# A complex mix of heads and the second step of a forward transform: fp32 matmuls against three fp16 passes of high and low halves

## The reference, cut to what matters

```python
xf = jnp.fft.fft2(x)
qf = xf.reshape(b, HEADS, hd, h * w)
qn = _l2norm_lastdim(qf)
attn_f = jnp.einsum('bhcn,bhdn->bhcd', qn, qn) * temp_f[None]
attn_f = jax.lax.complex(jax.nn.softmax(attn_f.real, axis=-1), jax.nn.softmax(attn_f.imag, axis=-1))
out_cplx = jnp.einsum('bhcd,bhdn->bhcn', attn_f, qf)
out_f = jnp.abs(jnp.fft.ifft2(out_cplx)).reshape(b, c, h, w)
g = jax.nn.sigmoid(_conv(g, w2, b2))
out_f_l = jnp.abs(jnp.fft.ifft2(g * xf))
```

## Time and profile before

| | |
|---|---|
| median of 3 runs | 26842.19 us (26841.0 to 26844.8) |
| the profiled execution | 26840.82 us, of which the span is 26839.0 us |
| PE busy | 23909.5 us (89%) |
| DVE busy | 19661.7 us (73%) |
| ACT busy | 13616.0 us (51%) |
| granted clock of TensorE, mean | 0.939 |

### The profile page before, as it was taken

One profiled execution on the slowest core, in us unless ns is written; L12 is line 12 of the kernel. 1 busy time (PEld: TensorE's weight loads), 2 busy tenths in 40 slices (PEclk: granted clock), 3 DMA queues, 4 the chain that ended last, 5 costly groups with the idle time before them and its releaser, 6 DMA issues. The chain is left out here.

```text
span 26839.0 us, 328765 instructions
## 1 busy us (share of the span) xinstructions
PE 23909.5 (89%) x108001; PEld 14269.1 (53%) x108001; DVE 19661.7 (73%) x22753; ACT 13616.0 (51%) x19703; POOL 12340.1 (46%) x4613
## 2 busy tenths in 40 slices
PE   6988989889898998989988888888888888888888
PEld 4776867768677676877733333333333333333333
DVE  3562635537255372644699999999999999999999
ACT  1413223131321413214277777777777777777777
POOL 0000000000000000000099999999999999999998
PEclk7998989989898998989999999999999999999999
DMA  1121121211202112021244444444444444444444
GB/s 53 49 76 61 33 65 38 76 61 42 66 32 73 61 55 69 27 66 57 75 178 165 193 165 173 183 167 191 169 169 185 169 191 166 167 189 167 190 168 163
DMA packets 816277, 3112.23 MB, mean 116 GB/s; under 512 B 61865, under 2 KB 325434, under 8 KB 530362
## 3 DMA queue, kind: packets, MB, share of 16 engines
q1 hardware_dynamic: 815802, 3106.12, 31.1%
HBM read 2813.61 MB, written 292.30 MB: 116 GB/s over the span
## 5 line engine op out<-in xcount | busy, mean ns | idle before, releaser
L2176 POOL TENSOR_TENSOR hid<-hid,bc 128x2048 f32<-128x2048 f32 x2048 | 7814.6, 3816 | 909.2 <-DVE carry L2082 906.5
L1845 PE MATMUL yp<-hid,ident 128*128 128x512 f32 x16384 | 7344.7, 597 | 430.7 <-POOL hid L2176 430.7
L2150 POOL TENSOR_SCALAR_AFFINE_SELECT ident<-ident 128x128 f32<-128x128 f32 x1 | 0.3, 294 | 13331.3 <-DVE ident L2035 13331.3
L1845 PEld LDWEIGHTS yp<-hid,ident 128*128 128x128 f32 x16384 | 3039.7, 189 | 4628.3 <-issue 3957.9
L2068 DVE TENSOR_TENSOR_SCAN hid<-da,carry,t 128x512 f32<-128x512 f32 x3968 | 4857.8, 1266 | 111.0 <-DVE carry L2082 7.7
L2074 DVE TENSOR_TENSOR_SCAN hid<-t,carry,hid 128x512 f32<-128x512 f32 x3968 | 4828.1, 1258 | 29.2 <-ACT t L1916 28.5
L2169 POOL TENSOR_TENSOR hid<-bc,du 128x1024 f32<-128x1024 f32 x2048 | 4101.4, 2003 | 197.0 <-PE yp L1845 170.6
L1066 PE MATMUL bk<-region 128*128 128x256 f16 (+2 forms) x32688 | 3946.9, 279 | 24.6 <-ACT region L1365 19.1
L1066 PEld LDWEIGHTS bk<-region 128*128 128x128 f16 (+2 forms) x32688 | 3400.0, 119 | 603.9 <-issue 175.8
L1916 ACT ACTIVATE t<-delta,v_a 128x512 f32<-128x512 f32 x4096 | 2660.0, 681 | 1574.0 <-DVE hid L2074 1570.9
L1801 PE MATMUL pj<-xn,w_x 128*128 128x512 f32 x4096 | 2376.5, 734 | 1079.2 <-ACT xn L1941 1031.0
(11 more groups left out here) (272 smaller groups left out, 24892.0 us busy)
## 6 DMA issues: line engine op xcount, KB each, us to landing
bc<-bc_rows SPq DMA_DIRECT2D x1024, 2048.0 KB, 7.2
work<-in_shift_d SPq DMA_DIRECT2D x256, 512.0 KB, 3.5
xpad<-in_x SPq DMA_DIRECT2D x32, 2048.0 KB, 18.8
work<-in_x SPq DMA_DIRECT2D x128, 512.0 KB, 4.8
gated<-work SPq DMA_DIRECT2D x256, 256.0 KB, 2.2
region<-gated SPq DMA_DIRECT2D x256, 256.0 KB, 2.9
region<-heads SPq DMA_DIRECT2D x256, 256.0 KB, 3.1
region<-in_x SPq DMA_DIRECT2D x256, 256.0 KB, 3.6
```

Of the source, the lines that this page charges most:

```text
L1845: m = nc.tensor.matmul(yp[:, h, :], ident[:, :], hid[:, k % 4, n, :], start=False, stop=(g == G - 1 and n == 3), skip_group_check=True)
L2176: nc.gpsimd.tensor_tensor(hid[:, k % 4, :, :], hid[:, k % 4, :, :], bc[:, g, 1, :, :], ALU.mult).then_inc(s_hc.sem, 1)
```

## The change

An fp32 value, scaled by a power of two, is split into an fp16 high half and an fp16 low half (value less high half), and a product is made of three passes: high by high, weights high by data low, weights low by data high.

In the forward transform, ScalarE's copy to `AB` makes the high half; VectorE makes the low half by `ab_low` (one scalar_tensor_tensor from PSUM), ahead of `xi_copy` in each step. Stage1 and stage2 wait for the low half. Stage2 does 12 fp16 matmuls for 4 fp32 ones, with tables split once in the setup (`dft`). The copies to `XR` and `XI` scale back.

In the heads stage, ScalarE's shifted real copy and VectorE's shifted imaginary one make high halves (`imh` is the count of the latter), and VectorE makes both low halves. The copy of the turned rows moves from ScalarE to VectorE, between the lows and `add_squares`. The mix does 12 fp16 matmuls for 4 fp32 ones, with `mix16` split once per image; the squares scale back.

The diff, cut to its core (semaphore declarations are left out):

```diff
@@ -42,6 +42,8 @@
+HSCALE, HWEIGHT = 128.0, 16384.0
+ASCALE, CSCALE = 16.0, 16384.0
@@ -193,7 +195,9 @@
-        AB = wk(4096, 1024).rearrange("p (s c u) -> p s c u", s=2, u=P)
+        AB = wk(4096, 1024).bitcast(F16).rearrange("p (s h c u) -> p s h c u", s=2, h=2, u=P)
+        ab_flat = wk(4096, 1024).bitcast(F16).rearrange("p (s h n) -> p s h n", s=2, h=2)
+        dft = sb("dft16", [P, 2, 3 * P], F16)
@@ -203,7 +207,8 @@
-        shifted = [wk(1024 + 2048 * i, 1024) for i in range(2)]
+        shifted = [wk(1024 + 2048 * i, 1024).bitcast(F16).rearrange("p (c s n) -> p c s n", c=2, s=2) for i in range(2)]
+        mix16 = wk(10240, 3 * P).bitcast(F16).rearrange("p (i s o) -> p i s o", i=3, s=2)
@@ -407,6 +412,10 @@
+                    for i, part in enumerate((k["cs"], k["sc"][:, 0:P])):
+                        of_i = slice(2 * P * i, 2 * P * i + (2 - i) * P)
+                        link(nc.vector.tensor_scalar(dft[:, 0, of_i], part, CSCALE, None, ALU.mult))
+                        link(nc.vector.scalar_tensor_tensor(dft[:, 1, of_i], part, CSCALE, dft[:, 0, of_i], ALU.mult, ALU.subtract))
@@ -712,8 +723,14 @@
                 def xi_copy(t):
...
-                    V.tensor_copy(XLAST[:, 1, 4 * t:4 * t + 4], spectrum[:, :, U64])
-                    V.tensor_copy(XI[:, 4 * t:4 * t + 4, :], spectrum[:, :, 0:U64]).then_inc(s_xi.sem, 1)
+                    back_by = 1.0 / (ASCALE * CSCALE)
+                    V.tensor_scalar(XLAST[:, 1, 4 * t:4 * t + 4], spectrum[:, :, U64], back_by, None, ALU.mult)
+                    V.tensor_scalar(XI[:, 4 * t:4 * t + 4, :], spectrum[:, :, 0:U64], back_by, None, ALU.mult).then_inc(s_xi.sem, 1)
+
+                def ab_low(t):
+                    dve.wait_ge(s_s1.sem, s_s1.at(b, t + 1))
+                    dve.wait_ge(s_ab.sem, s_ab.at(b, t + 1))
+                    V.scalar_tensor_tensor(ab_flat[:, t % 2, 1], bk[t % 2][:, :], ASCALE, ab_flat[:, t % 2, 0], ALU.mult, ALU.subtract).then_inc(s_abl.sem, 1)
...
                 def columns(i):
@@ -722,9 +739,12 @@
                 columns(0)
+                ab_low(0)
                 columns(1)
...
                     for t in range(4 * i, 4 * i + 4):
+                        if t + 1 < NK:
+                            ab_low(t + 1)
...
                         columns(i + 2)
@@ -779,6 +799,8 @@
+                link(V.tensor_scalar(mix16[:, :, 0], mix_t[:, :, :], HWEIGHT, None, ALU.mult))
+                link(V.scalar_tensor_tensor(mix16[:, :, 1], mix_t[:, :, :], HWEIGHT, mix16[:, :, 0], ALU.mult, ALU.subtract))
@@ -795,6 +817,12 @@
+                def turned_rows(kk):
+                    dve.wait_ge(s_tr.sem, s_tr.at(b, kk + 1))
+
+                    dve.wait_ge(s_sh.sem, s_sh.at(b, kk))
+                    V.tensor_copy(turned, bk[0][:, :]).then_inc(s_trc.sem, 1)
+
                 def add_squares(kk):
@@ -802,10 +830,17 @@
                 def body(kk, par):
...
-                    V.tensor_copy(shifted[par][:, 512:], bk[2][:, :]).then_inc(s_shi.sem, 1)
+                    V.tensor_scalar(shifted[par][:, 1, 0], bk[2][:, :], HSCALE, None, ALU.mult).then_inc(s_imh.sem, 1)
+                    dve.wait_ge(s_shr.sem, s_shr.at(b, kk + 1))
+                    V.scalar_tensor_tensor(shifted[par][:, 0, 1], bk[1][:, :], HSCALE, shifted[par][:, 0, 0], ALU.mult, ALU.subtract)
+                    dve.wait_ge(s_imh.sem, s_imh.at(b, kk + 1))
+                    V.scalar_tensor_tensor(shifted[par][:, 1, 1], bk[2][:, :], HSCALE, shifted[par][:, 1, 0], ALU.mult, ALU.subtract).then_inc(s_shi.sem, 1)
+                    if not (isinstance(kk, int) and kk == NK - 1):
+                        turned_rows(kk + 1)
...
+                turned_rows(0)
@@ -1094,20 +1129,22 @@
                 def stage1(t):
...
-                    pe.wait_ge(s_ab.sem, s_ab.at(b, t - 1))
+                    pe.wait_ge(s_abl.sem, s_abl.at(b, t - 1))
...
                 def stage2(t):
-                    pe.wait_ge(s_ab.sem, s_ab.at(b, t + 1))
+                    pe.wait_ge(s_abl.sem, s_abl.at(b, t + 1))
...
-                    A, Bm = AB[:, t % 2, :, 0:HALF], AB[:, t % 2, :, HALF:]
-                    for o, (ca, cb_) in ((bk[2 + t % 2], (k["cs"][:, 0:P], k["cs"][:, P:])), (bk[4 + t % 2], (k["sc"][:, 0:P], k["cs"][:, 0:P]))):
+                    COS, NSIN, SIN = 0, P, 2 * P
+                    for o, (ca, cb_) in ((bk[2 + t % 2], (COS, NSIN)), (bk[4 + t % 2], (SIN, COS))):
...
-                        mm(o3, ca, A, start=True, stop=False)
-                        m = mm(o3[:, :, 1:64], cb_, Bm, start=False, stop=True)
+                        for wh, ph in ((0, 0), (0, 1), (1, 0)):
+                            mm(o3, dft[:, wh, ca:ca + P], AB[:, t % 2, ph, :, 0:HALF], start=(wh == 0 and ph == 0), stop=False)
+                        for wh, ph in ((0, 0), (0, 1), (1, 0)):
+                            m = mm(o3[:, :, 1:64], dft[:, wh, cb_:cb_ + P], AB[:, t % 2, ph, :, HALF:], start=False, stop=(wh == 1))
@@ -1195,11 +1232,11 @@
-                    re, im = shifted[par][:, 0:512], shifted[par][:, 512:]
-                    mm(o_re, mix_t[:, 0, :], re, start=True, stop=False)
-                    mm(o_re, mix_t[:, 2, :], im, start=False, stop=True)
-                    mm(o_im, mix_t[:, 0, :], im, start=True, stop=False)
-                    mm(o_im, mix_t[:, 1, :], re, start=False, stop=True).then_inc(s_o.sem, 1)
+                    for o, terms in ((o_re, ((0, 0), (2, 1))), (o_im, ((0, 1), (1, 0)))):
+                        for n_, (w_, part) in enumerate(terms):
+                            for wh, ph in ((0, 0), (0, 1), (1, 0)):
+                                m = mm(o, mix16[:, w_, wh, :], shifted[par][:, part, ph, :], start=(n_ == 0 and wh == 0 and ph == 0), stop=(n_ == 1 and wh == 1))
+                    m.then_inc(s_o.sem, 1)
...
                 def body(kk, par):
@@ -1380,13 +1417,14 @@
                 def xr_copy(t):
...
-                    cp(XLAST[:, 0, 4 * t:4 * t + 4], spectrum[:, :, U64])
-                    cp(XR[:, 4 * t:4 * t + 4, :], spectrum[:, :, 0:U64]).then_inc(s_xr.sem, 1)
+                    back_by = 1.0 / (ASCALE * CSCALE)
+                    cp(XLAST[:, 0, 4 * t:4 * t + 4], spectrum[:, :, U64], scale=back_by)
+                    cp(XR[:, 4 * t:4 * t + 4, :], spectrum[:, :, 0:U64], scale=back_by).then_inc(s_xr.sem, 1)
...
                 for t in range(NK):
...
-                    cp(AB[:, t % 2, :, :].rearrange("p c u -> p (c u)"), bk[t % 2][:, :]).then_inc(s_ab.sem, 1)
+                    cp(ab_flat[:, t % 2, 0], bk[t % 2][:, :], scale=ASCALE).then_inc(s_ab.sem, 1)
@@ -1433,18 +1471,12 @@
-                def turned_rows(kk):
-                    act.wait_ge(s_tr.sem, s_tr.at(b, kk + 1))
-
-                    act.wait_ge(s_sh.sem, s_sh.at(b, kk))
-                    cp(turned, bk[0][:, :]).then_inc(s_trc.sem, 1)
-
                 def squares(kk, par):
...
-                        cp(sq2[s], bk[3 + 2 * par + s][:, :], ACT.Square).then_inc(s_os.sem, 1)
+                        cp(sq2[s], bk[3 + 2 * par + s][:, :], ACT.Square, scale=1.0 / (HSCALE * HWEIGHT)).then_inc(s_os.sem, 1)
...
                 def root(kk):
@@ -1455,15 +1487,12 @@
-                    cp(shifted[par][:, 0:512], bk[1][:, :]).then_inc(s_shr.sem, 1)
-                    if not (isinstance(kk, int) and kk == NK - 1):
-                        turned_rows(kk + 1)
+                    cp(shifted[par][:, 0, 0], bk[1][:, :], scale=HSCALE).then_inc(s_shr.sem, 1)
...
-                turned_rows(0)
```

More of the change, by code:

```diff
@@ L530, in layer0 @@
         s_gst = sem("s_gn_stored")
-        LINKS = 128
+        LINKS = 130
         v = count("s_dve_link", LINKS)
@@ L537, in layer0 @@
         s_s1 = count("s_stage1", NK)
-        s_ab = count("s_stage1_copied", NK)
+        s_ab = count("s_stage1_high", NK)
+        s_abl = count("s_stage1_low", NK)
         s_s2 = count("s_stage2", NK)
@@ L588, in layer0 @@
         s_shi = count("s_shifted_imag_copied", NK)
+        s_imh = count("s_shifted_imag_high", NK)
         s_o = count("s_heads_mixed", NK)
@@ L648, in _ @@
         def _(dve):
-            credit(dve, v, s_shi, s_xhn, s_xi, s_h1c, s_gx, vq, vf, s_pq, s_lq, s_pf, s_lf, s_ud, s_y, s_fd, s_ms, s_bvc, s_oa, s_x1, s_bn)
+            credit(dve, v, s_abl, s_shi, s_imh, s_trc, s_xhn, s_xi, s_h1c, s_gx, vq, vf, s_pq, s_lq, s_pf, s_lf, s_ud, s_y, s_fd, s_ms, s_bvc, s_oa, s_x1, s_bn)
             V = nc.vector
@@ L1363, in _ @@
         def _(act):
-            credit(act, a, s_row, s_hq, s_hf, s_last, s_sq, s_tt, s_trc, s_shr, s_xn, s_ab, s_xr, s_t8c, s_rel, s_sig, s_z, s_abs, s_uc, s_mc, s_os, s_of)
+            credit(act, a, s_row, s_hq, s_hf, s_last, s_sq, s_tt, s_shr, s_xn, s_ab, s_xr, s_t8c, s_rel, s_sig, s_z, s_abs, s_uc, s_mc, s_os, s_of)
             cp = lambda o, i, f=ACT.Copy, **kw: nc.scalar.activation(o, i, f, **kw)
```

## The result

The changed kernel takes 27,021.3 us (median of 4 runs, 27,012.1 to 27,027.2) where the kernel before took 26,843.5 (median of 4) in the same comparison: a ratio of 1.0066, 95% interval 1.0053 to 1.0079. It is slower by 0.66%, 178 us; the forecast was 27,040.

What follows compares the result with a forecast made beforehand. TensorE was taken to bound the forward stage, nearly throughout, and ScalarE with VectorE's add the heads, TensorE just behind. 26,840.8 + 91 (ring, start, tail) + 90 (clock) + 17 (heads) + 1.5 (setup) = 27,040 us, range 26,900 to 27,200.

Steps and rivals of the forecast that it cites:

- The ring: Forward stage: columns, low pass, stage2, stage1 and the next columns' load wait on each other, 13.24 us per four steps.
- 4 to 5 named as the sign of being right: Forward stage: one TensorE pause of 4 to 5 us for each columns, ended by VectorE's low pass.
- The later start of `columns(1)`: Forward stage's start: `ab_low(0)` stands ahead of `columns(1)` and waits for the first stage1 and its copy, 3.4 us later.
- The tail: Forward stage from columns 7 to its end: 22.3 us where 20.9 were, +1.5 us.
- The clock: Forward stage: TensorE's clock falls behind each pause, 1.6 us each, seven pauses by 8 images, +90 us (0 to +123).
- The heads: Heads stage: VectorE's four added operations eat the saving; step 6.25 us, +0.1, in all +17 us (-19 to +112).
- 6.15 to 6.4 named as the sign of being right: Heads stage: a step of 6.15 to 6.4 us, VectorE's four operations back to back.
- The small ones: Setup and per-image extras: four VectorE operations in the setup +1.5 us once; `mix16`, scales and weight loads nothing.
- the clock did not hold in the forward stage: Rival, forward stage: longer pauses leave the clock up, total 26,950 us; chance 0.22.
- did in the heads: Rival, heads stage: the clock falls there too, in a third of the steps, +270, total 27,310 us; chance 0.10.
- an fp16 matmul of 512 columns: Rival, heads stage's mix: fp16 doesn't pay at this width, step 7.3 us, +290, total 27,330 us; chance 0.03.
- TensorE set neither stage: Rival, both stages: TensorE sets them, total 26,520 us, or 26,714 if only the heads gain; chance for both 0.07.

Runs made afterwards that it cites:

- Third buffer: The changed kernel with three buffers for the columns instead of two: 26,919.4 us, ratio 1.0026 to the kernel before.
- GpSimd: The changed kernel with three buffers of columns and both operations of columns run on GpSimd: 26,814.3 us, ratio 0.9987 to the kernel before.
- the pause filled: The changed kernel with 22 unused fp16 matmuls of 384 columns queued on TensorE ahead of stage2(4i+5): 26,955.4 us, ratio 1.0041 to the kernel before.

## Why the prediction was right

- **The ring closed where it was said to**, and with the forecast's links and lengths: low pass 0.68 (0.69 forecast), ring 13.3 with the clock up (13.24). The pauses after the first are 3.3 to 4.2 us, where 4.4 was forecast and 4 to 5 named as the sign of being right. Third buffer and GpSimd took the ring apart link by link.
- **The later start of `columns(1)`** came to 3.7 us (3.4 forecast: the columns are 8.26 us apart for 4.54). The tail with the pause filled is 22.7 us in the two images in which the clock held (22.3 forecast, though its own terms add to 22.2), and the tail before was 21.4, not 20.9, since the window of the earlier trace rows ends half a microsecond early. With 13.24 us for each of the six rings, these terms come to 92 us by the traces, for +91.
- **The clock** was taken at 1.6 us for each of seven pauses, +90; the traces give 94. The five later rings have a mean of 14.97 us, 1.7 over 13.24, 69 us in all, and the two kinds of ring with a third buffer differ by 1.64. The first of the seven pauses cost nothing (a ring of 13.2; it is only 1.8 to 2.5 us long). The tail, 25.8 us for 22.7, cost 3.1, 24 us in all: in seven of the eight images the clock falls in it twice, behind the pause of the ring and again behind the last `normalise`, as in the second image:

```profile
2034.05 2.29 PE L1101 MATMUL bk<-work,dft 128*128 128x260 f16 x12 [2.41 <-DVE work L733]
```

That the sum came out owes something to luck: the pause that cost nothing and the second fall in the tail, neither of them foreseen, all but cancel. The row of a pause of 3.87 us in the other layer was the right one to price the long pauses by; the forward stage's own pauses of 1.2 us were not. The Trainium skill ("TensorE: Matmul & The Clock Gate", section "HAM oscillation — how this bites in real kernels") tells of a kernel in which each wait for a DMA let the clock fall, in every turn of its loop. The trace agrees for the six later pauses of an image, of 3.3 to 4.2 us: the clock was at 0.50 behind each of them, in all 8 images.

- **The heads**: 6.06 us a step for 6.12, where +0.1 was forecast and 6.15 to 6.4 named as the sign of being right. The bare sum was 6.16 against 6.15; the 0.1 was a reserve for waits between VectorE's operations, and there are none: they start 0.60 us apart, less than the 0.62 summed, and the add starts 0.05 us earlier than before. That term was mis-sized by 27 us (+17 forecast, -10 measured), inside its bounds.
- **The small ones** stayed small: no stage but these two moved by much.
- **The rivals** fell by the traces: the clock did not hold in the forward stage, and did in the heads (1.00 in the window of 170 us above); an fp16 matmul of 512 columns costs half of one fp32 matmul record of 0.43 us (28 records of mix and shift take 4.54 us, the shift's 16 alone 1.95, which leaves 0.22 each for the 12); and TensorE set neither stage.
- **A row read for another**: the price of 0.110 us for an fp16 matmul of 256 columns was taken from a row of weight loads (PEld). It holds, by luck of loads and matmuls taking turns: 12 of them take 1.34 us to the next start at full clock, 0.112 each.

## What to carry to other kernels

An operation added on a side engine costs its place in the queue, not its length: 0.68 us behind a wait for a load closed a ring of 13 us that took in the load itself. Before making the busiest engine's work cheaper, follow each loop round once and sum the others; where one is level with it, the saving is worth nothing until that loop is shortened, and the same change that loses 0.66% here gains 0.64% once it is. In a loop on ScalarE look for table loads that a set loaded ahead of it would spare.

## What the runs showed of the hardware that was not expected

- The clock fell behind pauses of 2.59 us with a third buffer, in most but not all rings (13.33 and 11.69 us), and behind the 2.41 us of a `normalise` in some places and not in others, while 1.2 us cost nothing. When it falls, the three groups of matmuls behind the pause pay, 1.6 us in all.
- Feeding TensorE 3.6 us of useless matmuls in each pause of the ring made the program 66 us faster.
- GpSimd does the columns' operation in 3.61 us where VectorE takes 2.29; with the fp16 passes it was the cheaper place all the same (94.4 us for 109.6), with fp32 it was not (100.7 for 98.9, with a third buffer as well).
- VectorE starts operations from PSUM 0.60 us apart that last 0.68 to 0.69, even where each waits for a count that is already there.
